# The fourth batch's shared expert moves from behind the expert tiles to ahead of them

## The reference, cut to what matters

```python
x = x + ga * _L1_attn_ref(h, ...)
h = _layernorm(x, axis=-1) * (1 + cb) + sb
# inside _L1_ffn_ref, on h:
topk_w, topk_idx = lax.top_k(softmax(h @ gate_w.T), 2)      # then normalized: cw
for e in range(8):                                          # routed
    g, u = split(h @ w1[e]); moe += cw[:, e] * (silu(g) * u @ w2[e])
shared = (silu(h @ sw1.T) * (h @ sw2.T)) @ sw3.T            # every token
x = x + gb * (moe + shared)                                 # the output
```

## Time and profile before

| | |
|---|---|
| median of 3 runs | 1146.12 us (1146.06 to 1146.46) |
| the profiled execution | 1145.18 us |
| its span in the profile | 1143.5 us |
| PE busy | 1060.2 us (93%) |
| DVE busy | 895.2 us (78%) |
| ACT busy | 736.2 us (64%) |
| POOL busy | 334.6 us (29%) |
| PE's granted clock, mean | 0.97 of full speed |

### The profile page before, as it was taken

How to read it: one execution, slowest core, us unless ns; L and a number is a source line. 1 busy time by engine, 2 the same in 40 slices (tenths; PEclk the granted TensorE clock), 3 DMA queues, 4 the chain that set the end, 5 groups by cost and what they waited for, 6 DMA issues and landing times. The chain is left out here.

```text
span 1143.5 us, 22333 instructions
## 1 busy us (share of the span) xinstructions
PE 1060.2 (93%) x7536; PEld 923.7 (81%) x7536; DVE 895.2 (78%) x1817; ACT 736.2 (64%) x1399; POOL 334.6 (29%) x335
## 2 busy tenths in 40 slices
PE   5888888879999999999999999999999997979996
PEld 4656666658899899899898898898998986769994
DVE  5788988857788788788788788788788787867775
ACT  4679797767766666666666666666666654625661
POOL 3353544442311201211111111111111234753440
PEclk9889999979999999999999999999999998989999
DMA  7210001010401311311311211221221291824436
GB/s 256 94 52 16 16 6 44 14 50 23 137 21 50 112 47 47 108 45 52 100 51 53 94 58 53 89 62 53 80 71 54 83 45 66 355 98 116 123 98 234
DMA packets 67881, 92.13 MB, mean 81 GB/s; under 512 B 22658, under 2 KB 46338, under 8 KB 66787
## 3 DMA queue, kind: packets, MB, share of 16 engines
q1 hardware_dynamic: 64402, 81.83, 24.6%
q0 software_dynamic: 3408, 9.39, 2.2%
HBM read 46.35 MB, written 42.75 MB: 78 GB/s over the span
## 5 line engine op out<-in xcount | busy, mean ns | idle before, releaser
L1551 PE MATMUL all_psum<-all_h_parts,attn_wp 128*128 128x512 f32 x1140 | 297.6, 396 | 0.0
L1551 PEld LDWEIGHTS all_psum<-all_h_parts,attn_wp 128*128 128x128 f32 x1140 | 209.8, 189 | 39.7
L1723 ACT CAST attn_pp<-attn_p 128x512 fp32r<-128x512 f32 (+3 forms) x256 | 117.4, 459 | 187.8 <-DVE attn_p L1831 185.7
L1812 DVE TENSOR_TENSOR attn_pp<-attn_p,attn_pp 128x512 fp32r<-128x512 f32 (+3 forms) x256 | 198.0, 773 | 6.5 <-ACT attn_pp L1723 6.5
L1970 POOL TENSOR_TENSOR all_gate<-all_gate,attn_sq 128x512 f32<-128x512 f32 x64 | 84.7, 1324 | 369.8 <-ACT attn_sq L1734 369.7
L1630 PE MATMUL all_psum<-attn_qkp 128*128 128x512 f32 (+3 forms) x768 | 164.9, 323 | 3.7 <-DVE attn_qkp L1812 3.7
L1577 PE MATMUL all_psum<-attn_pp,attn_vp 128*128 128x512 f32 (+3 forms) x768 | 163.8, 322 | 1.0 <-DVE attn_pp L1812 0.5
L1577 PEld LDWEIGHTS all_psum<-attn_pp,attn_vp 128*128 128x128 f32 x768 | 129.4, 189 | 21.6 <-issue 1.2
L1630 PEld LDWEIGHTS all_psum<-attn_qkp 128*128 128x128 f32 x768 | 124.8, 190 | 12.6 <-issue 4.3
L1831 DVE TENSOR_TENSOR attn_p<-all_psum,attn_mask 128x512 f32<-128x512 f32 (+3 forms) x256 | 123.5, 482 | 2.1 <-PE all_psum L1630 0.9
L1054 DVE TENSOR_REDUCE front_top<-all_psum 128x2 f32<-128x256 f32 (+3 forms) x128 | 99.4, 815 | 17.8 <-PE all_psum L695 16.8
(11 more groups left out here) (381 smaller groups left out, 1899.5 us busy)
## 6 DMA issues: line engine op xcount, KB each, us to landing
expert_rows<-attn_empty SPq DMA_DIRECT2D x8, 2080.0 KB, 12.7
expert_weight_parts<-all_wraw SPq DMA_DIRECT2D x32, 304.0 KB, 2.4
experts_wx<-expert_weight_parts SPq DMA_DIRECT2D x8, 1216.0 KB, 16.6
all_wraw<-in_w1p SPq DMA_DIRECT2D x8, 1024.0 KB, 5.9
all_yacc<-expert_rows SPq DMA_DIRECT2D x39, 130.5 KB
all_wraw<-in_wx SPq DMA_DIRECT2D x16, 304.0 KB, 3.0
attn_mask<-decay_masks SPq DMA_DIRECT2D x16, 256.0 KB, 2.6
all_x<-in_x SPq DMA_DIRECT2D x4, 512.0 KB, 7.0
```

Of the source, the lines that this page charges most:

```text
L1551: last = nc.tensor.matmul(out, wp[:, a, k, col:col + P], hh[:, c, k, b * S:(b + 1) * S], start=(m == 0), stop=(m == 5))
L1723: nc.scalar.copy(pp[:, u % 2, 0, cols], p[:, cols]).then_inc(p_hi, 1)
L1812: nc.vector.tensor_tensor(out, whole, high.bitcast(F32), ALU.subtract).then_inc(ready, 1)
```

## The change

Chunks 6 and 7 are done in the first part, ahead of the tiles, with their own `output(3)`; nothing of the shared expert is left after the tiles. The waits ahead of the tiles ask for 8 chunks in place of 6 and for 4 multiplies in place of 3, and the identity matmuls of the tail start their own accumulation. The tail's start keeps the two matmuls that put x into `X_BANK`.

```diff
-        LATE = FS * (B - 1)
+        SHARED = FS * B
...
-                                                    stop=(f == FS - 1 and m == 2 and tt % 2 == 1 and b < B - 1))
+                                                    stop=(f == FS - 1 and m == 2 and tt % 2 == 1))
...
                 down(3)
                 ups(5)
                 down(4)
+                gates(6)
+                ups(6)
                 down(5)
+                gates(7)
+                ups(7)
+                down(6)
+                down(7)
...
-                pe.wait_ge(upd_done, B - 1)
+                pe.wait_ge(upd_done, B)
                 pe.wait_ge(rows_read, 2 * B)
-                pe.wait_ge(hid_done, LATE)
+                pe.wait_ge(hid_done, SHARED)
...
-                gates(LATE)
-                ups(LATE)
-                gates(LATE + 1)
-                ups(LATE + 1)
                 pe.wait_ge(t_hid, TILES)
...
-                down(LATE)
-                down(LATE + 1)
...
-                                                start=(i == 2 and c == 0), stop=(c == 1))
+                                                start=(c == 0), stop=(c == 1))
...
                 high(4)
                 silu(5)
                 high(5)
+                silu(6)
+                high(6)
+                silu(7)
+                high(7)
...
-                            act.wait_ge(down_done, LATE)
+                            act.wait_ge(down_done, SHARED)
...
-                            act.wait_ge(hid_done, LATE)
+                            act.wait_ge(hid_done, SHARED)
...
-                silu(LATE)
-                silu(LATE + 1)
-                high(LATE)
-                high(LATE + 1)
...
                 hide(5)
                 lower(4)
                 lower(5)
+                hide(6)
+                lower(6)
                 output(2)
+                hide(7)
+                lower(7)
+                output(3)
...
-                dve.wait_ge(hid_turned, TILES)
-                hide(LATE)
-                hide(LATE + 1)
-                lower(LATE)
-                lower(LATE + 1)
```

## The result

| | before | after |
|---|---|---|
| median, first series (6 runs each) | 1146.72 us | 1151.53 us (1150.27 to 1154.29) |
| median, second series (29 and 6 runs) | 1145.73 us | 1150.81 us (1149.07 to 1152.45) |
| profiled execution, its span | 1145.18, 1143.5 | 1152.31, 1150.6 |

The changed kernel is slower: the ratio is 1.0048 (95% interval 1.0038 to 1.0059), which is 5.5 us (the two medians of that series lie 4.8 us apart), and 1.0044 (1.0030 to 1.0058), 5.0 us, in the second series. The forecast was 1152.0 us, which is 5.9 us on top of the 1146.12 us that the kernel before had at the time.

What follows compares the result with a forecast made beforehand. PE was taken to bound the tiles, transfers the tail until 1132.1 us, then DVE. The exposed chain's +7.55 and the faster tile start's -1.65 gave +5.9 on 1146.12: 1152.0 us, range 1149.0 to 1155.2.

Steps and rivals of the forecast that it cites:

- The exposed chain: Ahead of the tiles: chunks 6 and 7 on PE and DVE move hidden_of(0) from 1028.65 to 1036.2, +7.55 us.
- The add of output(3): On DVE ahead of tile 0's split: ends at 1035.7, and only then may DVE split the tile.
- The tail gives nothing back: After the tiles: the late work lies beside scatter and reload of results, so removing it gains 0.
- The bound of 1 us for an earlier sum of part 0: Tail, DVE's first sum: upper bound of the gain, at most 1 us or so; taken as 0.
- The start of the tiles: First three tile steps at 2.4 GHz take 5.5 us in place of 7.20: -1.65 us.
- A: The forecast: chain of chunks 6 and 7 exposed, tiles start at 2.4 GHz; 1152.0 us, chance 0.45.
- B: Start of the tiles: short holes together leave 1.2 GHz, first steps again 7.20 us; +7.55, 1153.7 us, chance 0.25.
- Rival D: First part: clock doesn't fall at 1017 or rises sooner, saving 2.3 us at down(4) and gates(6); +3.6, 1149.7, chance 0.13.
- Rival C: Tail: clock falls and delays L2646 and the last pair, +2.8 us more; 1154.8 us, chance 0.10.
- Rival E: First part: new work fits PE's holes if gates(6) starts in the hole from 1014.62; 1144.5 us, chance 0.07.

Runs made afterwards that it cites:

- the first trace: Profiled execution of the changed kernel, nothing else changed: 1152.31 us, span 1150.6.
- the last experiment: Changed kernel reordered: PE passes ahead of downs, DVE hides ahead of adds, and tile 0 turned and split before output(3)'s multiply: 1143.73 us, 0.9982 to before.
- the order alone: Changed kernel with only chunks 5 to 7 reordered: PE's passes ahead of the downs, DVE's hides ahead of the adds: 1.0007 to before.
- the handover: Changed kernel where PE turns tile 0 right behind down(7), DVE splits it before output(3)'s multiply and adds that output after the tiles: 1.0027 to before.
- the second trace: Changed kernel run and traced once more, nothing else changed: 1.0044 to before, trace span 1148.0 us.
- the warm-start one: Kernel before with 11 matmuls without use between down(5) and the first transpose: 0.9993 to before.
- the one filled in both places: Kernel before with 8 matmuls without use behind down(5) and 8 more in the tail: 0.9991 to before.

## Why the prediction was right, and where it was off

**The exposed chain.** Forecast against the first trace: `hide(6)` 1024.9 and 1025.17, multiply of `output(2)` 1027.0 and 1027.16, `hide(7)` 1029.5 and 1029.55, `down(7)` 1031.6 and 1031.66, first transpose 1034.5 and 1034.82, `hidden_of(0)` 1036.2 and 1036.43. +7.55 was +7.78. Each link came from a row of the same operation, and the order from the lists; that is why it held. That it was order and not work is shown by the last experiment, which does the same work, and the order alone gives back 4.2 us of the 5.0.

**The add of output(3)** was given 1.2 us of the chain, from 1034.5 to 1035.7. In the trace the split would have had to wait for ACT's copy until about 1035.6 anyway, so the add alone held it for some 0.2 us. The sum was right since both end there. What the handover gains (1.6 us in its trace) is that the multiply and the wait for it went too.

**The tail gives nothing back.** Shown by leaving the chunks out (0.9998) and by doubling their passes (1.0006). The bound of 1 us for an earlier sum of part 0 was not used either: that sum waits 9.61 us for its transfer in the changed kernel.

**The start of the tiles** is the term that was mis-sized: -1.65 was booked for 2.4 GHz through three steps (5.5 in place of 7.20 is -1.70 by its own figures), and -0.86 was measured in the first trace, since the clock fell after `hidden_of(0)`; in the second trace, where it was down when `hidden_of(0)` started, they take 6.67 us, -0.53. A start at 2.4 GHz throughout is worth 1.66 to 1.88 (5.54 us in the reordered kernel, 5.32 with matmuls without use), so the price was right and the condition wasn't met. Whether the short holes are the cause is open: both traces of the changed kernel show the fall, and those of `gates(6)` ahead of `down(4)` and of the order alone, with the same holes from `down(7)` on, don't (5.33 and 5.32 us). The row from which the condition was taken, 1.66 and 3.19 us of the tail at 1.00, was one execution's luck: two later traces with such a tail show a fall in it, the warm-start one at L2649 and the one filled in both places at L2641, behind 1.99 us without matmuls. A and B were the ends, and the two traces lie between.

**Rival D** was given 0.13 as another course of things. It is what one of the two traces shows: the same instructions, the same hole of 3.31 us, and the clock up behind it in place of down. How many of the executions go that way isn't known, since only two were traced. Its price of 2.3 us was right (1036.43 to 1034.13 is 2.30, and 2.51 counted from the map). The first trace, with the clock down as in A, is 7.1 us longer than before, 1.2 above the forecast's 5.9: 0.8 from the start of the tiles, the rest from the chain and the tail. That the median came to 1151.5 and not above 1152.0 is then most likely owed to executions that took the course of D, which A left out. So the figure is right partly by luck, by two errors of opposite sign.

**Rival C** fell for the changed kernel. In all seven traces without late work in the tail PE does the four identity matmuls in 5.15 to 6.40 us, mostly at 1.2 GHz, and L2646's pair in 1.98. The rule of the Trainium skill ("TensorE: Matmul & The Clock Gate", "HAM oscillation — how this bites in real kernels") is borne out where PE waits 10.63 us (a mean of 0.74 over that wait, and 0.61 over the four matmuls behind it). In the warm-start trace L2649 ran at 1.2 GHz behind 3.05 us without matmuls too, but that wait was for DVE. The rule isn't borne out at L2646 of the changed kernel, which follows 6.03 us of matmuls. The prediction took the rule for one of every such gap; the waits in the section's own case are longer than the 1.66 us of the earlier trace rows, so that row doesn't speak against it. Rival E's condition was not met, and the reordered kernel shows what it needs.

What stays open: why the clock falls in one execution and not in another at the same hole was not tried, and the runs of a kernel are spread over 2.7 to 7.0 us in all series but one (1.2 us in the first six of before), of which the clock's falls may explain a part; a later start of the whole stage, as the 3.2 us in the order-only trace, is another part whose cause was not looked for. The handover alone would need more runs to be told from noise.

## What to carry to other kernels

Work that costs nothing under a transfer costs its whole chain of handovers where it is put ahead of a stage that is bound by an engine; before such a move, walk the chain link by link through every engine's list, from the first instruction that stands in a queue behind something else. If it must move, put its matmuls into the hole ahead of it and not behind the waiting instruction, and hand over to the next stage before the last clean-up, not after it. Where one trace shows TensorE's clock up behind a hole of 3 us, take both levels as possible and price both.

## What was not expected of the hardware

The granted clock behind the same hole of 3.31 us without matmuls was 0.50 in one traced execution and 1.00 in the other, and moved the start of the tiles by 2.3 us; so a single trace doesn't tell a kernel's clock. A tail in which PE works about half of the time, with gaps of 1.8 and 3.05 us, fell to 0.50 at the pair that matters in one trace and stayed at 1.00 in another (gaps of 1.66 and 3.19 us), at a price of 0.9 us in DVE's chain and perhaps as much again in the last stores, while a wait of over 10 us did no harm in the changed kernel: the clock was back during the matmuls right behind it, before that pair.
